# Attention projections of an LN, attention and FFN kernel as three one-pass products of high and low parts

## The reference

```
def attn(residual, W_key, W_query, W_values, W_output, Bias_*):   # residual [2, 2048, 256], W_* [16, 256, 64]
    keys    = einsum('bse,neh->bsnh', residual, W_key)    + Bias_key
    queries = einsum('bse,neh->bsnh', residual, W_query)  + Bias_query
    values  = einsum('bse,neh->bsnh', residual, W_values) + Bias_values
    scores  = einsum('bknh,bqnh->bnqk', keys, queries) / sqrt(64)
    scores  = where(q < k, 1e-10, scores)        # masked keys keep the score 1e-10, they are not dropped
    probs   = softmax(scores, axis=3)
    return einsum('bqnh,nhe->bqe', einsum('bnqk,bknh->bqnh', probs, values), W_output) + Bias_output
x = residual
x = x + attn(layernorm(x), ...)
x = x + ffn(layernorm(x), ...)       # 3 blocks: h += linear(gelu(LN(linear(h)))), int4 codes, scales and LoRA parts
```

## Time and profile before

| what | value |
|---|---|
| median of 3 runs | 2277.4 us |
| the profiled execution's own time, its span | 2273.86 us, 2272.0 us |
| TensorE busy | 2176.1 us (96%) |
| GpSimd, VectorE, ScalarE busy | 1359.2 us (60%), 1311.6 us (58%), 900.7 us (40%) |
| first stage, 0 to 92.2 us | TensorE busy 65.32 us, granted clock 0.82 |
| pair loop, 92.2 to 1878 us | TensorE busy 1761.79 of 1785.80 us, granted clock 1.00 |
| rest, 1878 to 2272 us | TensorE busy 348.98 of 394.00 us, granted clock 0.93 |
| DMA | 93.92 MB, 41 GB/s over the span |

### The profile page before, as it was taken

How to read it: one execution, slowest core, us unless ns; L and a number is a source line. 1 busy time by engine, 2 the same in 40 slices (tenths; PEclk the granted TensorE clock), 3 DMA queues, 4 the chain that set the end, 5 groups by cost and what they waited for, 6 DMA issues and landing times. The chain is left out here.

```text
span 2272.0 us, 37164 instructions
## 1 busy us (share of the span) xinstructions
PE 2176.1 (96%) x13152; PEld 1138.1 (50%) x13152; DVE 1311.6 (58%) x3583; ACT 900.7 (40%) x1764; POOL 1359.2 (60%) x1212
## 2 busy tenths in 40 slices
PE   6999999999999999999999999999999997899987
PEld 2344444445454545454444454444444556777764
DVE  6755555555555566565656565555555661456655
ACT  2244444444444446444444444444444440110111
POOL 1277777777777777787878777878787611111110
PEclk9699999999999999999999999999999997999998
DMA  1001010101010111111111111111110124311100
GB/s 45 18 13 49 18 49 17 50 17 49 18 49 17 49 54 31 36 32 35 33 34 33 33 34 33 36 31 37 30 38 22 45 70 144 139 65 47 65 19 19
DMA packets 117205, 93.92 MB, mean 41 GB/s; under 512 B 67552, under 2 KB 84128, under 8 KB 117024
## 3 DMA queue, kind: packets, MB, share of 16 engines
q1 hardware_dynamic: 117024, 91.55, 13.2%
HBM read 69.21 MB, written 21.76 MB: 40 GB/s over the span
## 5 line engine op out<-in xcount | busy, mean ns | idle before, releaser
L676 POOL TENSOR_TENSOR acc<-acc,probs 128x512 f32<-128x512 f32 (+1 forms) x900 | 1007.8, 1157 | 282.3 <-ACT probs L1026 282.2
L1026 ACT ACTIVATE probs<-ps_s 128x512 f32<-128x512 f32 (+1 forms) x1152 | 579.1, 576 | 566.5 <-PE ps_s L831 394.4
L1088 DVE TENSOR_REDUCE partial<-ps_bg 128x1 f32<-128x512 f32 x768 | 486.9, 683 | 143.8 <-PE ps_bg L763 143.8
L853 PE MATMUL ps_o<-probs,v 128*64 128x512 f32 (+3 forms) x2560 | 538.1, 541 | 0.0
L711 PE MATMUL ps_bg<-home,w_in 128*128 128x512 f32 x768 | 381.9, 620 | 17.9 <-DVE q_lo L1071 10.6
L823 PE MATMUL ps_s<-q_hi,k_hi 64*128 64x512 f32 (+3 forms) x1280 | 299.7, 460 | 0.0
L763 PE MATMUL ps_bg<-k_bf,q_bf 64*128 64x512 bf16 (+3 forms) x1280 | 281.0, 361 | 16.0 <-DVE partial L1085 3.4
L853 PEld LDWEIGHTS ps_o<-probs,v 128*64 128x64 f32 x2560 | 155.3, 136 | 231.3 <-issue 184.1
L763 PEld LDWEIGHTS ps_bg<-k_bf,q_bf 64*128 64x128 bf16 x1280 | 78.0, 93 | 376.9 <-issue 333.1
L1085 DVE CUSTOM_DVE_ANT_0 junk<-ps_bg,mask_q 128x512 bf16<-128x512 f32 (+3 forms) x512 | 230.2, 484 | 41.2 <-issue 40.1
L829 PE MATMUL ps_s<-q_hi,k_lo 64*128 64x512 f32 (+3 forms) x1280 | 239.0, 362 | 0.0
(11 more groups left out here) (124 smaller groups left out, 2065.2 us busy)
## 6 DMA issues: line engine op xcount, KB each, us to landing
e<-masked_weights SPq DMA_DIRECT2D x128, 128.0 KB, 3.0
scale<-inverse_sums SPq DMA_DIRECT2D x128, 128.0 KB, 2.9
heads_turned<-num SPq DMA_DIRECT2D x64, 256.0 KB, 2.0
c_o_in<-heads_turned SPq DMA_DIRECT2D x6, 2048.0 KB, 7.7
home<-in_L_attn_residual SPq DMA_DIRECT2D x8, 512.0 KB, 5.2
c_o_in<-heads_turned SPq DMA_DIRECT2D x8, 512.0 KB, 8.5
c_x_in<-in_L_attn_residual SPq DMA_DIRECT2D x8, 512.0 KB, 8.2
out<-c_y SPq DMA_DIRECT2D x8, 512.0 KB, 2.8
```

The costliest lines, as they stand in the source:

```text
L676: g.tensor_tensor(acc[h][:, group % 2, q0:q0 + w], acc[h][:, group % 2, q0:q0 + w], probs[h][:, probs_slot(i, t), at:at + w], ALU.add).the ...
L853: mm = pe.matmul(ps_o[64 * h:64 * h + 64, q0:q0 + w], v[:, kb, 64 * h:64 * h + 64], probs[h][:, probs_slot(i, t), at:at + w], start=first, ...
L1026: nc.scalar.activation(probs[h][:, probs_slot(i, t), CH * half:end], ps_s[:, k % SCORE_BANKS, 0:end - CH * half], ACT.Exp, scale=SCORE_SCA ...
L1088: e.reduce_max(to, of, AX.X).then_inc(max_read, 1)
```

## The change

What it does, part by part:

- **Products.** The input and the weights are each split into a high part (rounded to fp32r) and a low part (the difference). A unit becomes six fp32r matmuls: for each half, high times high, high weight times low input, low weight times high input. `x_part` has two places of (high, low) x (two halves) x 512 for one chunk each; `w_hi` and `w_lo` are new tiles.
- **Making the parts.** ScalarE copies the turned chunk to the high part (`take_x`), VectorE subtracts (`x_low`); once per chunk and sequence. Once per pair ScalarE copies the weights (`weights_high`, at slot 64), and GpSimd subtracts (`weights_low`, at tile 12).
- **Loads.** After their making, the parts of a chunk are stored to DRAM (`keep_x`, 1 MB each), and for every later pair they are loaded again, chunk by chunk, into the two places (`load_parts`); place k%2 is loaded when the units of the chunk before it in that place are done.
- **Room.** `v_from` (the sums of values from a key on) moves into the second half of `home`; `masked_num` goes, the masked numerator is written straight into `num`; `max_rows` holds two chunks instead of four, `rows` two instead of four; `ones_row`, `mask_q` and `never_later` shrink. With that some waits and places in SyncE's order change (`install_max`), and the second sequence's chunks are normalised in the order 1, 0, 3, 2. The FFN's first four `lora_a` parts are loaded last (`load_la`).

```diff
+LN_CHUNKS = [PROJ_CHUNKS, [1, 0, 3, 2]]
-TURN_AT = {3: 76, 2: 82, 1: 102, 0: 108}
+TURN_AT = {1: 76, 0: 82, 3: 108, 2: 114}
+W_HIGH_AT = 64
+W_LOW_TILE = 12
...
+        w_hi = sb("w_hi", [P, halves, 3, P], F32R)
+        w_lo = sb("w_lo", [P, halves, 3, P], F32R)
+        x_part = sb("x_part", [P, 2, 2, halves, CH], F32R)
-        xs = home.rearrange("p (c s t) -> p c s t", c=4, s=halves)
...
+                def keep_x(batch, c):
+                    sp.wait_ge(xs_ready, START + xs_ready_count(batch, c))
+                    sp.dma_start(x_kept[batch, c], x_part[:, x_slot(c)].bitcast(F32)).then_inc(x_out[x_slot(c)], 16)
+
+                def load_parts(j, k):
+                    sp.wait_ge(proj_done, START + (NPROJ * j + 3 * (k - 1) if k >= 2 else NPROJ * (j - 1) + 3 * (k + 3)))
+                    sp.wait_ge(x_out[k % 2], START + 32 * (j // n_pairs + 1))
+                    sp.dma_start(x_part[:, k % 2].bitcast(F32), x_kept[j // n_pairs, PROJ_CHUNKS[k]]
+                                 ).then_inc(x_in[k % 2], 16)
...
                 def install_max(j, c):
-                    if j:
-                        sp.wait_ge(pv_done, START + NT * (j - 1) + LAST_TILE[c] + 1)
-                    sp.wait_ge(row_kept, START + 16 * (nth(j, c) + 1))
+                    if c < 2:
+                        sp.wait_ge(s_ready, START + tile_end(j, LAST_TILE[c + 2]))
+                    elif j:
+                        sp.wait_ge(s_ready, START + tile_end(j - 1, LAST_TILE[c - 2]))
+                    sp.wait_ge(row_kept[c % 2], START + kept_count(j, c))
...
+                def weights_low(j):
+                    pool.wait_ge(w_high, START + j + 1)
+                    g.tensor_tensor(w_lo[:, :, :, :], w_in[:, :, :, :], w_hi[:, :, :, :].bitcast(F32), ALU.subtract
+                                    ).then_inc(w_ready, 1)
...
                 def project(j, u):
                     c, m = PROJ_CHUNKS[u // 3], u % 3
+                    k = u // 3
                     if u == 0:
-                        pe.wait_ge(w_loaded, START + 144 * (j + 1))
-                    if m == 0:
+                        pe.wait_ge(w_ready, START + j + 1)
+                    if m == 0 and (j == 0 or j % n_pairs == 0 and k < 2):
                         pe.wait_ge(xs_ready, START + xs_ready_count(j // n_pairs, c))
+                    elif m == 0:
+                        pe.wait_ge(x_in[k % 2], START + 16 * (2 * (j - 1) + k // 2 + 1 - j // n_pairs))
                     bank_read("proj", j, u)
-                    for s in range(halves):
-                        mm = pe.matmul(bank("proj", j, u), w_in[:, s, m, :], xs[:, c, s, :],
-                                       start=(s == 0), stop=(s == halves - 1))
+                    products = [(w_of, z, s) for s in range(halves) for w_of, z in ((w_hi, 0), (w_hi, 1), (w_lo, 0))]
+                    for n, (w_of, z, s) in enumerate(products):
+                        mm = pe.matmul(bank("proj", j, u), w_of[:, s, m, :], x_part[:, k % 2, z, s, :],
+                                       start=(n == 0), stop=(n == len(products) - 1))
                     mm.then_inc(proj_done, 1)
...
+                def weights_high(j):
+                    act.wait_ge(w_loaded, START + 144 * (j + 1))
+                    act.wait_ge(proj_done, START + NPROJ * j)
+                    nc.scalar.copy(w_hi[:, :, :, :], w_in[:, :, :, :]).then_inc(w_high, 1)
...
+                def x_low(batch, c):
+                    k = LN_CHUNKS[batch].index(c)
+                    for s in range(halves):
+                        dve.wait_ge(x_high, START + x_high_count(batch, c, s))
+                        low = e.tensor_tensor(x_part[:, k % 2, 1, s, :], turned(batch, c, s),
+                                              x_part[:, k % 2, 0, s, :].bitcast(F32), ALU.subtract)
```

More of the change, by code:

```diff
@@ L279, in attention @@
             "p (l g) -> p l g", g=D // 16)
-        w_t = [xs[:, l // 2, l % 2, :] for l in range(n_layers)]
+        w_t = [home[:, l * CH:(l + 1) * CH] for l in range(n_layers)]
         ps_s = ctx.enter_context(nc.psum_tensor("ps_s", [P, SCORE_BANKS, CH], F32))
@@ L303, in attention @@
         xs_ready = sem("xs_ready")
+        x_high = sem("x_high")
+        x_out = [sem(f"x_out{b}") for b in range(2)]
+        x_in = [sem(f"x_in{b}") for b in range(2)]
+        w_high = sem("w_high")
+        w_ready = sem("w_ready")
+        la_loaded = sem("la_loaded")
         ffn_w_loaded = sem("ffn_w_loaded")
@@ L331, in attention @@
         above_ready = sem("above_ready")
-        row_kept = sem("row_kept")
+        row_kept = [sem(f"row_kept{b}") for b in range(2)]
         e_ready = sem("e_ready")
-        e_kept = sem("e_kept")
+        e_kept = [sem(f"e_kept{b}") for b in range(2)]
         e_sq_in = sem("e_sq_in")
@@ L493, in _ @@
                     load_x(0, c)
+                for c in PROJ_CHUNKS:
+                    keep_x(0, c)
                 sp.wait_ge(consts, START + 2)
+                load_parts(1, 0)
+                load_parts(1, 1)
                 load_weights(1)
-                for k, (kind, c) in enumerate(FIN_FIRST):
+                for kind, c in FIN_FIRST:
                     if kind == "mt":
@@ L510, in _ @@
                     spread_masked(i, 3)
+                    if more:
+                        load_parts(i + 1, 2)
                     if i:
@@ L514, in _ @@
                     spread_masked(i, 2)
+                    if more:
+                        load_parts(i + 1, 3)
                     if i:
@@ L531, in _ @@
                         keep_masked(i + 1, 3)
-                    if more:
-                        install_max(i + 1, 3)
                     spread_masked(i, 0)
+                    install_max(i, 0)
                     masked_rows(i, 2)
+                    if next_batch(i) is not None:
+                        for c in LN_CHUNKS[next_batch(i)][2:4]:
+                            load_x(next_batch(i), c)
+                        for c in LN_CHUNKS[next_batch(i)][0:2]:
+                            keep_x(next_batch(i), c)
                     store_heads(i, 3)
@@ L557, in _ @@
                         keep_masked(i + 1, 0)
+                    if next_batch(i) is not None:
+                        for c in LN_CHUNKS[next_batch(i)][2:4]:
+                            keep_x(next_batch(i), c)
+                load_la()
                 spread_inverse(N - 1, 1)
@@ L641, in normalise @@
                                     ).then_inc(o_ready, 1)
+                weights_low(1)
                 for i in range(N - 1):
@@ L651, in _ @@
                             masked_denominators(i)
+                        if t == W_LOW_TILE and i + 2 < N:
+                            weights_low(i + 2)
                         for c in (1, 0):
@@ L812, in scores @@
                     q = slice(CH * group + q0, CH * (group + 1))
+                    of_rows = max_rows[:, group % 2, q0:CH]
                     diagonal = kb // 4 == group
@@ L830, in scores @@
                                   skip_group_check=True)
-                    last = [pe.matmul(out[h], max_gate[HEAD[h], :], max_rows[HEAD[h], q], start=False,
+                    last = [pe.matmul(out[h], max_gate[HEAD[h], :], of_rows[HEAD[h], :], start=False,
                                       stop=not diagonal, skip_group_check=True) for h in range(2)]
@@ L834, in scores @@
                         for part in range(2):
-                            last = [pe.matmul(out[h][:, 64 * part:64 * part + 64], never_later[HEAD[h], h, part, :],
+                            last = [pe.matmul(out[h][:, 64 * part:64 * part + 64], never_later[HEAD[h], part + 1 - h, :],
                                               ident_bf[HEAD[h], 64 * h:64 * h + 64], start=False, stop=(part == 1),
@@ L1005, in _ @@
                     evacuate(0, kind, c, k + 1)
+                weights_high(1)
                 def exponentials(i, t, n):
@@ L1045, in _ @@
                                 evacuate(pair_of(i, kind, c), kind, c, fin_before(i, k) + 1)
+                        if n == W_HIGH_AT and i + 2 < N:
+                            weights_high(i + 2)
                         for c in PROJ_CHUNKS:
@@ L1253, in _ @@
                                 chunk_stats(next_batch(i), c)
+                            if next_batch(i) is not None and n == TURN_AT[c]:
+                                x_low(next_batch(i), c)
                         if i == N - 1 and n % 6 == 1 and n // 6 <= LAST_TILE[1]:
```

170 lines of the change are left out of this document (101 added, 69 removed).

## The result

| | before | changed kernel |
|---|---|---|
| median, same chip | 2275.0 us | 2352.5 us (2348.95 to 2355.88, 4 runs) |
| span of the profiled execution | 2272.0 us | 2350.6 us |
| from the start to the first scores | 92.2 us | 100.4 us |
| one pair of the loop | 113.34 us | 119.28 us |

The changed kernel is slower: ratio 1.0345, 95% interval [1.032, 1.037]. The forecast was 2210 us with a range of 2195 to 2245, so it was wrong, in sign too, and the range does not hold the time. One of the four runs of the kernel before took 7177.97 us and is left out of the ratio; the other three lie between 2271.89 and 2277.4 us.

The account below looks back on a forecast made before the run. The loop was taken as bound by TensorE, busy 111.89 of 113.34 us a pair. Terms -74.5 + 1.5 + 0 + 1.5 + 3.2 + 3 + 1 = -64.3 us on 2273.86 gave 2210 us, range 2195 to 2245.

Parts of the forecast that it names:

- unit: TensorE's 180 projection units in the loop: six products of 0.216 us, 1.50 us instead of 1.91, -74.5 us.
- `weights_low`: GpSimd's subtraction once per pair, 2.2 us: covered before the denominators, so 0; at most 2.2 x 15 = 33 us.
- scan with its new operand: VectorE's scan with a one-column operand keeps its shape: 0.
- ScalarE's chain, row of maxima: ScalarE's chain between units adds idle time, +1.5 us; the maxima's row in SyncE's queue before the next scores, +1.5 us.
- `weights_high`, `load_parts`: ScalarE's weight copy once per pair, 1.0 us, fits free time: 0; 60 loads less 2 on mostly idle DMAs: 0.
- first stage: Before the loop: the first unit waits for VectorE's low parts, later units give some back; +3.2 us (0 to +8).
- pair 6: Eight more subtractions on VectorE, 6 us, and three banks occupied longer; half beside other work: +3 us (0 to 6).
- end: The lora_a parts are loaded last and TensorE waits for them before the first turned weight: +1 us (0 to 6.4).
- the forecast's signs: What would show it: units of 1.50 us, pairs about 108.6 us, no TensorE wait above 1 us for the sums.
- Rival 2: The covers fail: GpSimd's 0.2 us, SyncE's 0.5 us and ScalarE's chain, three times 15 us, 2255 us; chance 0.10.
- Rival 1: In the unit, steps of 0.23 us or a little more, or a slower entry: 2225 us, 2236 at 0.24; chance 0.13.
- Rivals 3 and 4: 3: the unit's weight loads not hidden, 2417 us, chance 0.04; 4: full-array fp32r no single pass, 2440 us, chance 0.02.

Follow-up runs that it names:

- experiment 5: experiment 4 with a unit again as four plain f32 products of the high parts alone, low parts left out of the result; 2288.3 us, ratio 1.0084.
- experiments 2, 3: 2: kernel before with the scan's ones as one f32 column, ratio 1.0022; 3: changed kernel with that column in bf16, ratio 1.0327.
- experiment 4: Changed kernel with `weights_low` moved from ahead of tile 12 to behind the sums of all tiles; 2234.3 us, ratio 0.983.
- experiments 1 and 3: 1: kernel before with one added GpSimd 128x768 subtraction at tile 12, 2395.1 us; 3: changed kernel with the scan's one column in bf16, 2347.7 us.

## Why the prediction was wrong

Term by term, each against the trace of the changed kernel or the experiment that isolates it:

| step | forecast | measured |
|---|---|---|
| unit | 1.50 us, -74.5 us | 1.58 us, -59 (54 in experiment 5) |
| `weights_low` | 0 (up to 33) | +125 |
| scan with its new operand | 0 | 0 (experiments 2, 3) |
| ScalarE's chain, row of maxima | +3.0 | 0 |
| `weights_high`, `load_parts` | 0 | 0, no wait of TensorE for them |
| first stage | +3.2 | +8.2 |
| pair 6 | +3 on top of its shorter units | 121.12 us, where 120.36 less 12 x 0.33 is 116.4: +4.7 |
| end | +1 | -0.3 |

The measured column gives -59 + 125 + 8.2 + 4.7 - 0.3 = +78.6, which is the difference of the spans (the 125 is from the pairs' lengths of the changed kernel and of experiment 4, 8.6 to 10.4 us in each of the 13).

**The step that failed is the cost of `weights_low`.** The text asked one question of GpSimd's added time: which consumer of GpSimd's results becomes late. It looked at the sums of group 1 and found 1.98 us to spare, and in the 13 pairs that was right: TensorE never waits for them there. It waits for them once, 2.0 us in pair 6, which the forecast's signs ("none above 1 us for the sums") rule out; it is part of that pair's +4.7, and 2.1 us in experiment 4, where the subtraction stands behind the sums. The text took the 0.46 us pause in the same rows as slack that absorbs work. It was slack, and it was also the moment at which VectorE's scan got in; the row of the scan, 637.04 to 638.32, lay in the same stretch, and I had not drawn it. The upper end, 2.2 x 15 = 33, was no upper end either: it counted each added us once, while the actual price is the rest of GpSimd's stretch (7.3 us), less the little that the maxima can wait, plus the lower clock afterwards (some 3 us). No run varied the length of the added work, so how the price depends on it stays open. The collision could be seen in the term's own row: I took a sum of GpSimd at 5.83/4 = 1.46 us, but one of these four had waited for the scan; four take 4.93 us at 547.07 of the changed kernel, and `weights_low` took 1.82 us, not 2.2.

**Rival 2** (the covers fail) named GpSimd's cover but priced it at about 1 us a pair and put the wait before the sums. Its sign for the reader, "new idle time before ... L850", is what came; the size was off by a factor of about ten, so its 2255 was no warning.

**Rival 1** (steps of 0.23 us) was the true one for the unit. I took the nearer array form (0.216, f32) over the same data type (0.23, fp32r); the data type was the better neighbour. Experiment 4, which has this step and no collision in the loop, gives 2234, where this rival had 2225; its other costs are 16.7 us instead of 10.2. Rivals 3 and 4 fell: 188 ns loads are hidden under steps of 0.23 us, and there is one record a product (1152). The rule of the Trainium skill that a load overlaps only in other row groups (TensorE: Matmul & The Clock Gate, "What overlaps and what doesn't") does not hold for these rows either. The mis-sized unit cost the forecast 15 us (-59 instead of -74.5), the second largest miss.

**First stage**: the low parts' delay was foreseen, the collision of the normalising (1.6 us) was not, nor that the first input lands later: the first statistics start at 11.61 us, where they started at 9.29. The cause of that stays open. **Right** were: 0.60 us of idle time after a short tile stays (0.60 at 607.85), the loads of the parts cost nothing (58 of 1024 KB, 5.1 us each), and no row of maxima came late.

## What to carry to other kernels

Before adding an instruction to GpSimd, list the VectorE instructions with two SBUF operands or per-partition scalars that fall into its stretch, and ask in which pause of GpSimd they run. In these traces the ones that read one operand from PSUM kept their length beside GpSimd (the maxima's L1195 0.69 us, `take_numerator`'s L1220 0.68). A pause that nobody waits for can be the one that VectorE needs. Where work must be added, put it where VectorE has no such instruction due, or give GpSimd one wait for VectorE's: it cost 1.2 us and saved 8.5. The upper end of such a term is not the added work's length: here it was the rest of GpSimd's stretch and the clock afterwards.

## What the runs showed of the hardware

- A VectorE scan that meets GpSimd at work waited through seven GpSimd instructions (7.3 us) in the changed kernel, and as long in experiments 1 and 3. It did not always: the scan of chunk 0 met GpSimd too, and took 1.74 us in the changed kernel, getting in between two of its sums. The sum behind it took 2.21 us instead of 1.28. What lets the one in and not the other stays open; the pauses of 0.46 and 0.48 us shown above were enough.
- VectorE's four normalising instructions with per-partition mean and scale took 2.97 us instead of 1.38 beside a GpSimd subtraction of 1.80 us, and 1.38 again when the two were kept apart.
- After 6.70 us without work TensorE ran at a mean granted clock of 0.57 for 6.8 us, most of it at the lower level, 1.2 GHz: a wait of 6.7 us cost 9.9.
- fp32r products on the full 128x128 array take 0.23 us for 512 columns, with 188 ns loads hidden; two passes of plain f32 take 0.43.
